# Step lists of their own for the last rounds of a software pipeline: two graph layers, an attention layer and two layer norms on one core

## What is computed

```python
x = _layernorm(x + L0(x, adj, ...))
x = _layernorm(x + L1(x, adj, ...))
```

```python
scores = einsum('bhqd,bhkd->bhqk', q, k) / sqrt(HD) + beta * adj_e
probs  = softmax(where(adj_e > 0, scores, -9e15))
out    = einsum('bhqk,bhkd->bhqd', probs, v)
```

## Time and profile before

| what | value |
| --- | --- |
| time, median of 3 runs | 1866.24 us (1865.49 to 1866.89) |
| time of the profiled execution | 1864.76 us |
| its span | 1863.0 us |
| PE busy | 1731.2 us (93%) |
| DVE busy | 1555.4 us (83%) |
| ACT busy | 1267.5 us (68%) |
| POOL busy | 652.9 us (35%) |
| granted TensorE clock, mean | 0.977 |

### The profile page before, as it was taken

One profiled execution on the slowest core, in us unless ns is written; L12 is line 12 of the kernel. 1 busy time (PEld: TensorE's weight loads), 2 busy tenths in 40 slices (PEclk: granted clock), 3 DMA queues, 4 the chain that ended last, 5 costly groups with the idle time before them and its releaser, 6 DMA issues.

```text
span 1863.0 us, 39868 instructions
## 1 busy us (share of the span) xinstructions
PE 1731.2 (93%) x13120; PEld 1633.3 (88%) x13120; DVE 1555.4 (83%) x5383; ACT 1267.5 (68%) x3036; POOL 652.9 (35%) x777
## 2 busy tenths in 40 slices
PE   4899999999999999999999999999999999999963
PEld 4799899999999999999999999899999999999952
DVE  4578889888888988888998888898888889888865
ACT  3466767676767776676767676676767776767644
POOL 1223333343333334343334333333434333433331
PEclk9899999999999999999999999999999999999975
DMA  5157666767666666766676776666666667677555
GB/s 156 29 106 149 127 130 131 145 135 147 145 122 132 136 143 141 150 134 125 132 144 139 143 144 124 129 137 145 138 151 136 123 135 140 138 143 144 115 116 116
DMA packets 550036, 247.65 MB, mean 133 GB/s; under 512 B 423100, under 2 KB 549832, under 8 KB 549832
## 3 DMA queue, kind: packets, MB, share of 16 engines
q1 hardware_dynamic: 538928, 231.91, 61.9%
q10 hardware_dynamic: 10904, 13.20, 2.1%
HBM read 56.25 MB, written 12.58 MB: 37 GB/s over the span
## 4 chain that ended last, share of the span: by engine, by line
PE 61%; DVE 24%; ACT 9%; issue 3%; DMA 1%; SPq 1%; ACTq 0%; POOL 0%; DVEq 0%; POOLq 0%
PE bank_w L384 33%; PE bank_m L384 10%; PE bank_u L384 6%; PE bank_o L384 4%; DVE halves L890 4%; DVE bank_s L885 4%; PE bank_s L384 4%; ACT normed L632 2%; ACT bank_s L683 2%; DVE stats_y L851 2%; ACT halves L692 2%; DVE hlrl L792 2%; DVE normed L848 2%; PE bank_t L401 2%; DVE attTl L797 1%
## 5 line engine op out<-in xcount | busy, mean ns | idle before, releaser
L683 ACT ACTIVATE bank_s<-bank_s,hmin 128x256 f32<-128x256 f32 x768 | 311.1, 445 | 129.8 <-DVE hmin L885 114.1
L885 DVE CUSTOM_DVE_ANT_0 bank_s<-bank_s,bias_adj 128x256 f32<-128x256 f32 x768 | 308.1, 446 | 40.7 <-PE bank_s L384 40.4
L890 DVE TENSOR_TENSOR halves<-bank_s,halves 128x512 f16<-128x512 f32 x384 | 262.3, 683 | 27.4 <-ACT halves L692 24.3
L692 ACT ACTIVATE halves<-bank_s 128x512 f16<-128x512 f32 x384 | 228.6, 596 | 4.2
L384 PE MATMUL bank_w<-w_graph0h,hT_ach 128*128 128x384 f32 x576 | 201.5, 350 | 10.3 <-DVE w_graph0l L745 6.0
L384 PE MATMUL bank_w<-w_graph1h,hT_bh 128*128 128x384 f32 x576 | 200.1, 347 | 0.0
L384 PE MATMUL bank_o<-v_parts,pT 128*128 128x99 bf16 (+1 forms) x3072 | 186.7, 204 | 12.6 <-DMA pT<-halves 9.3
L384 PE MATMUL bank_w<-w_graph0l,hT_ach 128*128 128x384 f32 x576 | 195.6, 340 | 0.0
L384 PE MATMUL bank_w<-w_graph0h,hT_acl 128*128 128x384 f32 x576 | 195.3, 339 | 0.0
L384 PE MATMUL bank_w<-w_graph1l,hT_bh 128*128 128x384 f32 x576 | 195.0, 339 | 0.0
L384 PE MATMUL bank_w<-w_graph1h,hT_bl 128*128 128x384 f32 x576 | 194.6, 338 | 0.0
(11 more groups left out here) (177 smaller groups left out, 5327.3 us busy)
## 6 DMA issues: line engine op xcount, KB each, us to landing
x_in<-in_x SPq DMA_DIRECT2D x64, 384.0 KB, 3.7
adj_in<-in_adj SPq DMA_DIRECT2D x96, 256.0 KB, 3.6
q_st<-qk_hi SPq DMA_DIRECT2D x256, 96.0 KB, 2.3
k_st<-qk_hi SPq DMA_DIRECT2D x256, 96.0 KB, 2.3
q_st<-qk_lo SPq DMA_DIRECT2D x128, 96.0 KB, 2.2
k_st<-qk_lo SPq DMA_DIRECT2D x128, 96.0 KB, 2.2
out<-result ACTq DMA_DIRECT2D x32, 384.0 KB, 3.8
pT<-halves SPq DMA_TRANSPOSE x384, 3.1
```

The source lines that it names most:

```text
L683: nc.scalar.activation(bank[:, i * S:(i + 1) * S], bank[:, i * S:(i + 1) * S], ACT.Exp, bias=hmin[:, i, k:k + 1], scale=-1.0).then_inc(s_p ...
L692: nc.scalar.activation(halves[:, k % SPLIT, :, 0, :], bank_s[k % 2][:, :].rearrange("p (i s) -> p i s", i=NT), ACT.Copy).then_inc(s_pt_hi, 1)
L885: ve.tensor_tensor_reduce(bank_s[k % 2][:, i * S:(i + 1) * S], bank_s[k % 2][:, i * S:(i + 1) * S], bias_adj[:, i, :], -SCALE, BIG, ALU.ad ...
L890: ve.tensor_tensor(halves[:, k % SPLIT, :, 1, :], bank_s[k % 2][:, :].rearrange("p (i s) -> p i s", i=NT), halves[:, k % SPLIT, :, 0, :], ...
```

## The change

The rounds 0 to 32 stay as they were. Rounds 33 and 34 (35 was empty) become one body, whose steps each engine takes from a list of its own. Each list holds exactly the steps that the two rounds held before, in another order; no step is added or removed. Here `-1` is batch 30 and `+1` is the last norm of batch 31.

```diff
+LAST_ROUND = 1
+LAST = {
+    "pe": """
+        scores.7-1 attend.4-1 scores.8-1 attend.5-1 scores.9-1 attend.6-1 scores.10-1 turn_y.0-1 turn_y.1-1
+        attend.7-1 scores.11-1 turn_y.2-1 attend.8-1 q.0 attend.9-1 q.1 attend.10-1 attend.11-1 q.2 k.0 k.1
+        k.2 v.0 v.1 scores.0 scores.1 scores.2 scores.3 scores.4 attend.0 scores.5 attend.1 attend.2 scores.6
+        scores.7 attend.3 attend.4 scores.8 scores.9 attend.5 attend.6 scores.10 attend.7 scores.11 attend.8
+        attend.9 attend.10 attend.11""",
+    "act": """
+        weights.6-1 scores.7-1 weights.7-1 scores.8-1 b_norm2.0-1 weights.8-1 b_out.0-1 scores.9-1 turn_y.0-1
+        weights.9-1 scores.10-1 turn_y.1-1 weights.10-1 turn_y.2-1 scores.11-1 weights.11-1 q.0 q.1 q.2 k.0
+        k.1 k.2 c_norm.0 v.0 c_apply.0 v.1 c_store.0 scores.0 weights.0 scores.1 weights.1 scores.2 scores.3
+        weights.2 weights.3 scores.4 weights.4 scores.5 weights.5 scores.6 weights.6 scores.7 weights.7
+        scores.8 weights.8 scores.9 weights.9 scores.10 weights.10 scores.11 weights.11 c_norm.0+1 c_apply.0+1
+        c_store.0+1""",
+    "dve": """
+        scores.7-1 b_resid.0-1 weights.6-1 b_resid.1-1 scores.8-1 b_norm2.0-1 attend.5-1 weights.7-1 b_out.0-1
+        weights.8-1 scores.9-1 scores.10-1 turn_y.0-1 weights.9-1 turn_y.1-1 attend.7-1 scores.11-1
+        weights.10-1 turn_y.2-1 weights.11-1 q.0 attend.9-1 q.1 attend.11-1 q.2 k.0 c_stat.0 k.1 c_stat.1
+        c_norm.0 k.2 c_apply.0 v.0 v.1 scores.0 scores.1 weights.0 weights.1 scores.2 scores.3 weights.2
+        scores.4 weights.3 scores.5 attend.1 weights.4 weights.5 scores.6 scores.7 attend.3 weights.6
+        weights.7 scores.8 scores.9 attend.5 weights.8 weights.9 scores.10 attend.7 scores.11 weights.10
+        weights.11 attend.9 attend.11 c_stat.0+1 c_stat.1+1 c_norm.0+1 c_apply.0+1""",
+    "pool": """
+        b_apply.0-1 q.0 c_sum.0 q.2 v.0 v.1 c_sum.0+1""",
+    "sp": """
+        c_adj.0 weights.6-1 weights.7-1 weights.8-1 weights.9-1 weights.10-1 weights.11-1 q_stack.0 q_stack.1
+        k_stack.0 k_stack.3 k_stack.1 q_stack.2 k_stack.2 weights.0 weights.1 weights.2 q_stack.3 weights.3
+        weights.4 weights.5 weights.6 weights.7 weights.8 weights.9 weights.10 weights.11""",
+}
+
+def last_steps(engine, t):
+
+    steps = []
+    for word in LAST[engine].split():
+        name, _, k = word.partition(".")
+        steps.append((name, int(k.partition("+")[0].partition("-")[0]), t + int(k.lstrip("0123456789") or 0)))
     return steps
...
-            latest = max(int(word.partition("-")[2] or 0) for word in ORDER[order].split())
...
-            for t in range(NB + 3 + latest):
+            for t in range(NB + LAST_ROUND):
...
+            body(NB + LAST_ROUND, last_steps(order, NB + LAST_ROUND))
```

More of the change, by code:

```diff
@@ L109, in schedule @@
             steps.append((name, int(k), at))
+    return steps
+def last_steps(engine, t):
[3 more added lines that the diff above has]
+        steps.append((name, int(k.partition("+")[0].partition("-")[0]), t + int(k.lstrip("0123456789") or 0)))
     return steps
```

## The result

The changed kernel takes 1860.65 us (median of 8 runs, 1859.99 to 1863.49), the kernel before 1866.13 (8 runs). The ratio is 0.9973, 95% interval 0.9963 to 0.9984: by it the change is worth 5.0 us, somewhere from 3.0 to 6.9 (the two medians lie 5.5 apart). The forecast was 1861.0. The same program, timed again in a later set, gave 0.9980 (0.9971 to 0.9989). The profiled execution of the changed kernel has a span of 1858.3 against 1863.0.

The account below looks back on a forecast made before the run. No engine is full at the end; a chain of hand-overs for the last batch sets it. +0.3 front, -5.0 tail and -0.5 end sum to -5.2, so 1866.24 becomes 1861.0 us, range 1858.8 to 1864.8.

Parts of the forecast that it names:

- Front, +0.3: From batch 30's last heads to scores.0 of batch 31: scores.0 starts at 1815.1, 0.3 us later than before.
- the 0.25 charged for the store: Batch 30's output store, moved into the stack DMAs, was taken to delay scores.0 by 0.25 us, 1.1 at worst.
- Rival 1: PE from q.2 to k.2: clock stays low, +3.6 us, 1864.6; or POOL's late sum stalls k.2, 1 to 3; chance 0.17.
- Scores.3, -4.3: Tail, scores.0 to scores.3: 4.97 us instead of 9.25, k_stack.1 landing at 3.7 and scores.3 waiting for its bank.
- Scores.3 to scores.5, +2.2: Tail: ACT puts scores.3 ahead of weights.2, DVE scores.4 ahead of weights.3, so this takes 6.17 us against 3.93.
- From scores.5 on, -1.8 and -1.5: Tail: scores.5 to scores.7 takes 3.97 us against 5.75; the two turns to scores.11 take 8.65 against 10.18.
- issued at 6.05 and landed at 9.15 ... has cover until 9.8: First transpose, behind all seven stacks, counted from scores.0; ACT's weights.3 needs it, each us past 9.8 costs one.
- Rival 2: Tail keeps its old pace: last six heads take 5.3 a pair instead of 4.2, 3.3 us missing, 1864.3; chance 0.12.
- rival 3: More than forecast: clock high in part of the tail, or weights.3 through earlier, 2 us more, 1859; chance 0.06.
- Rival 4: Slower: late landings hold the three slots of halves and pT; from 1870 us; chance 0.03.
- the 5.1 that the prediction said a landing may take: Tail: three heads take 6.5 us, a slot needs its landing and 1.3, so transposes hide up to 5.1.
- End, -0.5: Last norm: c_stat.0 now precedes c_stat.1, so one statistics step goes under POOL's second half, winning 0.5 us.

Follow-up runs that it names:

- g1: Changed kernel with only batch 30's norm and its store put back between scores.1 and scores.2 on DVE and ACT; ratio to the kernel before 0.9985.
- e2: Changed kernel with only SP's order of batch 31's stacks and transposes put back; ratio to the kernel before 0.9996.
- e3: Changed kernel with the five lists up to scores.0 put back, batch 30's norm behind scores.1, except SP's stacks; ratio to the kernel before 1.0006.
- f2: f1 plus weights.2 ahead of scores.3 on ACT, weights.3 ahead of scores.4 on DVE, scores.6 ahead of attend.2 on PE; ratio to before 0.9976.
- f1: Changed kernel with the transposes of weights.0 and weights.1 moved ahead of k_stack.2 on SP; ratio to the kernel before 0.9980.
- f3: f2 with q_stack.3 moved behind the transpose of weights.4 on SP; 1859.95 us, ratio to the kernel before 0.9965.
- e4: Changed kernel with only the last norm's two statistics steps swapped back, half 1 first; ratio to the kernel before 0.9982.
- h1: Kernel before with only SP's order of batch 31's stacks and transposes changed to the new one; 1867.33 us, ratio 1.0011.
- x1: Changed kernel with 24 already met waits added on SP ahead of q_stack.0; ratio to the kernel before 0.9972.

## Why the prediction was right

**Front, +0.3.** From the start of round 33, q.0 was put at 14.2 (1799.7 less 1785.5) and came at 14.2 (1799.13 less 1784.91); q.2 at 19.5 and came at 19.5; q_stack.0 at 21.8 and went at 21.9; scores.0 at 29.6 and came at 29.4. What is missing is the 0.25 charged for the store: k_stack.0's third DMA went at 1811.99 and PE started at 1814.30, 2.31 later, where it was 2.35 before. The store could hardly touch that DMA: it was issued at 1813.23, 1.24 behind it. What the store cost stands further down SP's row, where the forecast charged nothing: the next stack DMA took 0.6 longer to issue and landed after 3.6, against 2.8 in g1, and the first transpose went 0.7 later than in g1. The Trainium skill, page DMA: Bandwidth & Descriptors, section Issuing engines are not separate DMA queues, says that the two engines' DMAs interleave, and the trace agrees. Rival 1 did not occur: the granted clock was 1.00 from 1804 on, and POOL's sum was done at 1809.19, 24.3 from the start of the round, where the forecast had 24.2.

**Scores.3, -4.3.** Forecast 4.97 behind scores.0, measured 5.06, and the wait is DVE's, not a DMA's. k_stack.1 itself landed 4.5 behind scores.0 and not 3.7, still ahead of the bank. From the start of the round, scores.3 comes at 34.5 in the changed kernel, at 38.0 with the old stacks (e2), at 37.2 with the old front (e3) and at 38.6 before: it takes both.

**Scores.3 to scores.5, +2.2.** Forecast at 11.14, measured 11.59. f2 shows that ACT's and DVE's order made the detour: without it 4.5 us instead of 6.5.

**From scores.5 on, -1.8 and -1.5.** Here the mechanism is right and a term is mis-sized. scores.7 was put at 15.11 and came at 16.06, scores.9 at 19.43 against 20.84, scores.11 at 23.76 against 25.06, the end of weights.11 at 28.0 against 29.3. The step is "issued at 6.05 and landed at 9.15 ... has cover until 9.8". The first transpose was issued at 6.86 (1821.16 less 1814.30), 0.7 of the delay being the store's by g1, and landed 3.3 later, at 10.1 and past the cover. The second was taken at the median of 3.1 and took 4.97. ACT's weights.4 therefore started at 13.3 (1827.61 less 1814.30). (The 6.05 counts from scores.0 at 1814.85; from the forecast's own 1815.1 it would be 5.8, and the miss is the greater.) f1 shows the first half of it: with both transposes issued earlier and landing near the median, scores.5 comes at 11.25 (forecast 11.14) and scores.7 at 15.41 (forecast 15.11). It shows as well that this alone is not kept, because the next transposes are then late. f3 ends its tail at 28.0, but that is not the forecast's 28.0: it has no detour and is 1.9 us ahead of the changed kernel at scores.5, and it loses half of that by scores.7, where it waits for a transpose. Rival 2, the old pace in the heads, did not occur: scores.7 to scores.11 took 9.0, forecast 8.65, before 10.18. Nor did rival 3: the granted clock was 0.52 from 1816 to 1844, and weights.3 was late. Rival 4 showed its mechanism in small, landings that hold the slots. They did so at 5.0, under the 5.1 that the prediction said a landing may take: that figure is for the steady turn of three heads, and the first transposes were issued late, behind the stacks.

**End, -0.5.** Measured 0.48 (15.17 to 14.69), and e4 gives 0.5 back.

**Sum.** Forecast -5.2. The last round of the profiled execution gained 4.1, the timed runs 5.0 with an interval of 3.0 to 6.9, which holds both. So the time came out 0.4 below the forecast while the tail was 1.3 above it: that the total fits better than its parts is chance, since executions of the same program differ by more than this (1859.99 to 1863.49).

**What the edits are worth.** They can't be added. Put back alone, the heads cost the round 3.4, the stacks 2.3, the front with the norm 4.8: some 10.5 together, for a gain of 4.1. Done alone, the stacks made the kernel slower (h1). Each part opens a wait that another closes: early stacks need an early k and q, the freed bank needs the new order of heads, and the norm has to leave the place where the wait for k_stack.1 had covered it.

## What to carry to other kernels

When the wait that a drain hangs on is taken away, list what stood in its cover and move that too; here one norm in its old place gave back 1.8 of 4.1 us. Change the order on all queues together, since a part by itself may be slower than nothing. Where a slot waits for a DMA, price its landing by the slowest of the view, not by the median (here 4.2 instead of 3.1, and even that was short of the 5.0 that came). A store that another engine issues has a price too: 0.7 us in the queue of stacks here. And compare two executions from a common mark: the same round started anywhere from 1784.8 to 1791.2 here.

## What the runs showed of the hardware that was not expected

In the changed kernel the landings of the transposes span 3.0 to 5.0 with a median of 3.1, and the 5.0 (4.97 and 4.99) stood in the same place in both profiles of it, so it belongs to the program and is no accident of one execution. The DMA view of the stretch from 1824 to 1826 lists one piece of the instruction queue, and in that from 1826 to 1828 the DMA engines move almost nothing for 1.2 us (GB/s in 40 slices of 0.05 us):

```profile
q8 instruction: 1, 0.02, 3.0%
```

```profile
GB/s 0 0 0 0 0 0 0 0 5 5 5 10 5 10 10 10 10 10 10 5 10 10 10 10 61 241 287 292 282 292 292 292 292 302 381 246 164 164 123 102
```

Every one of the thirteen profiles, that of the kernel before too, has one such piece of 16 KB behind scores.0, and in each a transpose issued within 3.1 us of it landed late: after 4.0 to 5.2 us (4.2 before, 5.2 in h1). In f1 SP took 2.75 us to issue that transpose instead of 1.25 to 1.3. x1 moved the piece, and the landings changed from 5.0 and 4.5 to 4.4 and 3.9, without coming down to 3.1. The crowd of stacks by itself does not make them late: in g1 and e3 the first two transposes stand right behind all seven stacks as well, the piece comes more than 5 us after them, and they landed after 3.1 to 3.3. This is still an association; that the fetch is the cause, and why the same piece costs 1.1 us in one kernel and 2.1 in another, stays open.
